# Relative attention on one Trainium2 core: each relative product in two halves of 64 queries

## The reference, cut to what matters

```
q = heads(xn @ Wq); k = heads(xn @ Wk); v = heads(xn @ Wv)      # 16 heads, depth 8, L = 512
r = heads(rel_pos_emb[idx] @ Wr)                                # 2L - 1 = 1023 relative positions
AC = einsum('bhld,bhmd->bhlm', q + u_bias, k)
BD = einsum('bhld,hrd->bhlr', q + v_bias, r)
score = (AC + _rel_shift(BD)) / sqrt(8)                         # shifted[l, m] = BD[l, m - l + L - 1]
attn = softmax(score); out = einsum('bhlm,bhmd->bhld', attn, v)
return out @ Wo + bo
```

## Time and profile before

| what | value |
|---|---|
| median of 3 runs | 1772.97 us (1772.47 to 1789.65) |
| the profiled execution | 1773.42 us, of which 1771.6 are the span from first to last instruction |
| mean granted TensorE clock over the span | 0.929 |
| spills of the relative stage issued | 128, from 1174.9 to 1643.0 us |

### The profile page before, as it was taken

How to read it: one execution, slowest core, us unless ns; L and a number is a source line. 1 busy time by engine, 2 the same in 40 slices (tenths; PEclk the granted TensorE clock), 3 DMA queues, 4 the chain that set the end, 5 groups by cost and what they waited for, 6 DMA issues and landing times. The chain is left out here.

```text
span 1771.6 us, 34092 instructions
## 1 busy us (share of the span) xinstructions
PE 1507.6 (85%) x11044; PEld 940.4 (53%) x11044; DVE 1237.8 (70%) x3765; ACT 1123.2 (63%) x2649; POOL 440.9 (25%) x444
## 2 busy tenths in 40 slices
PE   4698998989898864888888887579999999999855
PEld 2265555555555542666666666345454545454434
DVE  4477777777777755887888886637777777777543
ACT  1267777777777724777677675147887887887321
POOL 1333333333333224544545442110000000000010
PEclk9699999999999986999999998759999999999777
DMA  1687777777777740111011100049999998999200
GB/s 40 166 202 186 192 187 191 192 186 192 192 187 193 168 159 13 36 26 23 21 27 27 25 21 11 23 147 331 326 326 313 323 326 295 323 324 313 78 14 24
DMA packets 152798, 281.19 MB, mean 159 GB/s; under 512 B 25824, under 2 KB 29104, under 8 KB 152496
## 3 DMA queue, kind: packets, MB, share of 16 engines
q1 hardware_dynamic: 152624, 279.01, 54.5%
HBM read 148.03 MB, written 121.37 MB: 152 GB/s over the span
## 5 line engine op out<-in xcount | busy, mean ns | idle before, releaser
L519 ACT ACTIVATE a_Pm<-a_Pm,a_nm 128x272 f32<-128x272 f32 (+3 forms) x512 | 266.6, 570 | 162.5 <-DVE a_nm L441 162.3
L441 DVE CUSTOM_DVE_ANT_0 a_Pm<-ps,a_mask 128x272 f32<-128x272 f32 (+3 forms) x512 | 237.6, 502 | 86.8 <-PE ps L358 84.1
L1746 DVE CUSTOM_DVE_ANT_0 r_Sx<-ps,r_Sx 128x512 f32<-128x512 f32 x256 | 166.7, 689 | 150.6 <-PE ps L1627 150.5
L1696 ACT COPY r_BD<-ps 128x320 f32<-128x320 f32 x512 | 192.6, 425 | 84.9 <-PE ps L1617 81.5
L1617 PE MATMUL ps<-r_R,r_qv 32*128 32x320 f32 x1024 | 224.6, 501 | 5.9 <-DVE r_qv L1736 5.2
L1627 PE MATMUL ps<-r_K,r_qu 32*128 32x256 f32 x1024 | 224.8, 437 | 3.0 <-DVE r_nb L1746 3.0
L358 PE MATMUL ps<-a_Kst,a_Qst 128*128 128x272 f32 (+4 forms) x640 | 203.4, 413 | 12.1 <-DMA a_Kst<-bounce 11.6
L1703 ACT ACTIVATE r_Sx<-r_Sx,r_nb 128x512 f32<-128x512 f32 x256 | 182.8, 715 | 29.9 <-DVE r_nb L1746 23.5
L358 PEld LDWEIGHTS ps<-a_Kst,a_Qst 128*128 128x128 f32 x640 | 113.9, 192 | 140.8 <-issue 67.0
L1637 PE MATMUL ps<-m_ident,r_Sx 128*128 128x128 f32 x1024 | 172.0, 292 | 0.5 <-DVE r_PT L1755 0.5
L373 PE MATMUL ps<-m_ident,a_Pm 128*128 128x128 f32 x1280 | 169.8, 277 | 1.9 <-ACT a_Pm L519 1.2
(11 more groups left out here) (201 smaller groups left out, 2707.8 us busy)
## 6 DMA issues: line engine op xcount, KB each, us to landing
spill<-r_BD SPq DMA_DIRECT2D x128, 640.0 KB, 4.5
r_Sx<-spill SPq DMA_DIRECT2D x128, 512.0 KB, 5.3
a_Kst<-bounce SPq DMA_DIRECT2D x128, 264.0 KB, 4.7
a_Qst<-bounce SPq DMA_DIRECT2D x128, 256.0 KB, 4.7
bounce<-a_kh SPq DMA_DIRECT2D x32, 264.0 KB, 3.5
bounce<-a_kl SPq DMA_DIRECT2D x32, 264.0 KB, 4.0
bounce<-a_qh SPq DMA_DIRECT2D x32, 256.0 KB, 5.7
bounce<-a_ql SPq DMA_DIRECT2D x32, 256.0 KB, 6.0
```

Source lines behind the costliest of these rows:

```text
L441: nc.vector.tensor_tensor_reduce(out=Pm[:, u % 2, qt, 0:w], in0=S[:, S_of[qt]:S_of[qt] + w], in1=mask[:, N + AV - w:N + AV], scale=-SCALE, ...
L519: nc.scalar.activation(row, row, ACT.Exp, scale=-1.0, bias=nm[:, u % 2, qt:qt + 1]).then_inc(exp_done, 1)
L1696: nc.scalar.copy(BD[:, m % BUFS, j, HW * half:HW * half + HW], ps[:, BDB[k % 3], 0:HW]).then_inc(bd_ev, 1)
L1746: nc.vector.tensor_tensor_reduce(out=row, in0=ps[:, AC + n % 2, :], in1=row, scale=-SCALE, scalar=-BIG, op0=ALU.add, op1=ALU.min, accum_ou ...
```

## The change

The 128 queries of a relative product are split in two halves of 64, and each half has a range of its own: 64 queries need 512 + 64 = 576 columns (`BW`), two times 288. A matmul of 32 rows x 128 columns of the array and 320 columns long becomes two of 32 rows x 64 columns, 288 long, both into the same PSUM bank, one on partitions 0 to 63 and one on 64 to 127. ACT copies 288 columns instead of 320. The DRAM buffers keep a row pitch of 640 (`BP`). The spill of a pair becomes two transfers of 64 partitions, the rows of the second half placed 64 columns to the left of those of the first, relative to the shift, so that the skewed read-back stays as it was. The waits for a spill count 32 instead of 16.

```diff
-BW = N + P
+BW = N + 64
...
+    BP = N + P
...
-    spill = [nc.dram_tensor(f"spill{k}", (2, P, BW), F32, kind="Internal").ap() for k in range(SCRATCH)]
+    spill = [nc.dram_tensor(f"spill{k}", (2, P, BP), F32, kind="Internal").ap() for k in range(SCRATCH)]
...
-                    sp.dma_start(spill[k % SCRATCH].rearrange("t p n -> p t n"), BD[:, k % BUFS]).then_inc(wr[k % BUFS], 16)
+                    for a in range(2):
+                        rows = slice(64 * a, 64 * a + 64)
+                        dst = spill[k % SCRATCH]
+                        placed = bass.AP(tensor=dst.tensor, offset=64 * a * (BP - 1) + P - 64, ap=[[BP, 64], [P * BP, 2], [1, BW]])
+                        sp.dma_start(placed, BD[rows, k % BUFS]).then_inc(wr[k % BUFS], 16)
...
-                    sp.wait_ge(wr[m % BUFS], 16 * (m // BUFS + 1))
+                    sp.wait_ge(wr[m % BUFS], 32 * (m // BUFS + 1))
...
-                    skew = bass.AP(tensor=a.tensor, offset=P - 1, ap=[[BW - 1, P], [P * BW, 2], [1, N]])
+                    skew = bass.AP(tensor=a.tensor, offset=P - 1, ap=[[BP - 1, P], [P * BP, 2], [1, N]])
...
-                r0 = N - P - P * lt + HW * half
-                nc.tensor.matmul(ps[:, BDB[k % 3], 0:HW], qv[rows, n // QUAD % 2, P * lt:P * lt + P], R[rows, r0:r0 + HW],
-                                 start=True, stop=True).then_inc(bd_ready, 1)
+                for a in range(2):
+                    q0 = P * lt + 64 * a
+                    r0 = N - 64 - q0 + HW * half
+                    ins = nc.tensor.matmul(ps[64 * a:64 * a + 64, BDB[k % 3], 0:HW], qv[rows, n // QUAD % 2, q0:q0 + 64],
+                                           R[rows, r0:r0 + HW], start=True, stop=True)
+                ins.then_inc(bd_ready, 1)
...
-                    act.wait_ge(wr[m % BUFS], 16 * (m // BUFS))
+                    act.wait_ge(wr[m % BUFS], 32 * (m // BUFS))
```

## The result

The changed kernel takes 1897.9 us (median of 4 runs, 1886.0 to 1908.0) against 1776.7 before (4 runs): ratio 1.067, interval 1.058 to 1.075. The profiled execution took 1901.2 us, 1899.4 of them span, 127.8 more than before. I had forecast 1870, in 1830 to 1900.

The account below looks back on a forecast made before the run. TensorE was taken to bound pairs with values, DVE's loop those without. Lost overlap costs 97 us (56 pairs at 1.0, 67 at 0.61), other parts 0: 1773.4 + 97 = 1870 us, range 1830 to 1900.

Parts of the forecast that it names:

- Part 1: TensorE, relative heads: relative and content no longer overlap, 1.26 us a half for 0.74; +97 us over 123 pairs.
- The loop through DVE: Pairs without a values block: loop of DVE adds, transposes and content grows from 3.57 to 4.18 us, +0.61.
- The clock: TensorE's granted clock in the relative heads, read as 0.99 (2.4 GHz) before the change; no term in the sum.
- A: Relative heads: TensorE empties between the two shapes and sets the pace; 1870 us, own range 1856 to 1890, chance 0.64.
- Part 2: ACT's copies of 288 columns for 320: ACT stays behind TensorE, 0 us.
- Part 3: Two half spills at 227 GB/s: transfers 4.17 us a pair for 3.54, covered by TensorE's 4.41, 0 us.
- rival D: Relative heads: relative and content stay side by side, transfers keep over 278 GB/s; 6 us less, 1767 us, chance 0.10.
- Part 4: SP: one more issue of 0.36 us a pair, within 7 us of room, 0 us.
- B: Spills: shapes share the array but half-partition transfers set the pace, 0.48 us a pair; 1832 us, chance 0.14.
- C: Spills: rate falls to 167 GB/s, 5.10 us a pair, 173 us more; 1946 us, chance 0.06.
- E: Relative matmuls: column halves do not run side by side, +120 us on top of A; 1990 us, chance 0.03.

Follow-up runs that it names:

- experiment 3: Changed kernel with the content matmuls also cut in halves of 64 queries, so relative and content have one shape (32 x 64): 1753.3 us, ratio 0.988.
- experiment 5: Kernel before with only the content matmuls cut in two 32 x 64 tiles; relative stays 32 x 128, one spill: 1896.0 us, ratio 1.069.
- experiment 2: Kernel before with only the spill split in two 64-partition transfers: 1767.5, 1775.0, 1796.5 and 1800.8 us, against 1775.9 for the kernel before.
- experiment 1: Changed kernel with the spill again one transfer of 128 partitions and 576 columns: 1897.3 us, ratio 1.068.
- filled start: Changed kernel with four extra, never read matmuls in each of the first 19 pairs: 1876.8 us, ratio 1.059.

## Why the prediction was right or wrong

**Part 1, the shapes: right.** "TensorE empties between relative and content, and they no longer overlap": the rows show the second part, the overlap gone; blocks of 0.64 and 0.63 were measured for 0.63 and 0.63, 4.72 for 4.7 us in pairs with values. Experiments 3 and 5 show it from both sides: same halves and one shape, loss gone; no halves in relative and two shapes, loss back. TensorEngine Tiling (Array Packing) in the Trainium skill, section Tiling Modes, states the drain without a price and without saying whether it holds across row groups that are not shared. This case agrees with it across row groups that are not shared, at 0.12 to 0.20 us a change.

**The loop through DVE: 0.17 us too long.** I gave pairs without values 4.18 us; 4.01 was measured. The step "to the next first add at 1320.29 (0.21)" was carried over, and it is 0.03 when content is no longer beside a relative matmul that ends after it (1320.16 in the earlier trace rows; 1319.73 + 0.43). Experiments 3 and 5 agree: 0.19 us from the end of content to the add where the two kinds overlap (1531.68 to 1531.87), 0.04 where content runs after relative (1392.67 to 1392.71). Why the overlap delays the add is not shown. 67 x 0.17 = 11 us, less 56 x 0.04 = 2 by which pairs with values came out longer, which is why the overlap cost about 89 us and not 97.

**The clock: missing.** This is the step that failed. I read the clock of the stage from the earlier trace rows, 0.99, and took it for given. Nothing in the sum asked whether the granted clock would come up as early in the stage when the shapes differ; it stayed at its lower level up to the first values block, 86 us longer than before. 43 us in the profiled execution; without them it would have been at about 1858. That the median lies 28 us above my 1870 is this term, less the 8 us by which the overlap was priced too high, less the 5 us outside the intervals, and the median is 3 us below the profiled execution. It is 8 us outside the range that I gave to A itself, 1856 to 1890, and 2 us inside the whole range of 1830 to 1900. That it fell inside is luck: no term of the sum or of the range was for the clock.

**Part 2, copies: right** (nothing on the path). In experiment 3, where the path is shorter, the shorter ranges do count.

**Part 3, the transfers: right that they are covered, wrong in price.** 227 GB/s came from a copy that runs alone. Spill and read-back together, while busy, ran at 286 in the changed kernel and at 315 and 327 in experiments 2 and 3; I had expected 1,114,112 bytes in 4.17 us, 267. SBUF — State Buffer in the Trainium skill, section Door 1: The DMA port swizzle, has 64 partitions on half of the ports, at about 218 GB/s, and the sections behind it say that two transfers for the two halves serialize. An estimate from that page, with each transfer of a pair after the other: 1,114,112 bytes in 2.70 + 1.57 us, at most 261 GB/s. The longer hold of the DMA engines beside experiment 1 (share 0.90 for 0.77) agrees with the half of the ports; the 314 GB/s of experiment 3, idle time included, do not agree with the estimate. My sketch in rival D, that transfers in one queue drift apart over the engines, would explain it; the runs show the rate, not that cause. **Part 4, SP:** the issue takes 0.6 us and not 0.36, hidden all the same.

**Rivals.** B fell with experiment 1, where the spill is one transfer again and the time stays at 1897.3 us. C fell with the 286 GB/s of the changed kernel, E with its relative block of 0.64 us, too short for two halves one after the other (0.98). D had the transfers right and the tiles wrong.

## What to carry to other kernels

In this kernel tiles of TensorE overlap only with tiles of the same shape: when one kind of matmul is cut smaller, cut the kind that shares the array with it too, or leave both. Count the changes of tile shape in the inner loop, at 0.1 to 0.2 us each here, and do not carry the granted clock of a stage over to a changed order of matmuls: give it a term or a range of its own. A rate taken from one transfer alone is not the rate of a full queue (227 GB/s against 327 here).

## What the runs showed of the hardware

Two shapes that differ only in columns (32 x 64 and 32 x 128) and lie in different row groups do not run together; four tiles of one shape do, in two row groups and two column halves, next to four more of it. TensorE can have a matmul in flight for 110 us on end and stay at 1.2 GHz. In the kernels with two shapes (the changed one, experiments 1 and 5) the first values block ended that, in the filled start the eighth block of the filler; in the kernel before and in experiment 3, where relative and content overlap, the clock came up at 1199 and 1195 us with no such block. Two 64-partition spills with the read-back between them ran at 315 to 327 GB/s while busy at pairs of 3.5 to 3.7 us, at 286 at pairs of 4.0 and 4.7.
